# Six staging buffers in place of four for the weight loads of a gated attention block

## The chip, the core and the metric

The kernel runs on one core of a Trainium2 chip. The metric is the device time of one execution in microseconds (us). The engines are PE (TensorE, the matmuls; PEld is its weight load), DVE (VectorE), ACT (ScalarE), POOL (GpSimd) and SP (SyncE). In this kernel SP does no arithmetic: it issues every DMA, one after the other, and waits on semaphores between them.

## What is computed

A gated block on 16 sequences of 64 rows of 256 numbers: attention with 16 query heads in 4 groups of keys and values, and then a gated feed-forward part.

```python
x = x + tanh(g_xattn[0]) * xattn(layernorm(x), ctx, wq, wk, wv, wo, wk_ctx, wv_ctx, q_norm_w, k_norm_w)
x = x + tanh(g_ffn[0]) * ffn(layernorm(x), gate_w, up_w, down_w, gate_scale, up_scale, down_scale)

# xattn: B, L, T = 16, 64, 64; 16 heads of 128, 4 key/value groups
q = rope(rms_norm(x @ wq)); k = rope(rms_norm(x @ wk)); v = x @ wv
k_ctx = rms_norm(ctx @ wk_ctx); v_ctx = ctx @ wv_ctx
probs = softmax(q @ concat(k_ctx, k).T / sqrt(128) + causal mask)
out = (probs @ concat(v_ctx, v)) @ wo

# ffn: weights rounded to float8_e4m3 and back
fuse = silu((x @ gate_w) * gate_scale) * ((x @ up_w) * up_scale)
out = (fuse @ down_w) * down_scale
```

## The kernel before

**Tiles and steps.** Two sequences make a tile of 128 rows, so there are 8 tiles, and 4 steps for each (one group of 4 heads), 32 steps in all. A step number k counts from -6; what comes before step 0 fills the pipeline. Each engine has its own hand-written list of work, in the order of its `one_step`, and runs it strictly in that order; engines wait for one another on semaphores.

**Weights.** They come in 18 chunks, in the order of `CHUNKS`: chunk 0 to 2 are `kv` 0, 1, 2 (context keys, own keys, context values), 3 is `q` 0, 4 is `kv` 3 (own values), 5 and 6 are `q` 1 and 2, 7 is `o` 0, 8 is `q` 3, 9 is `gate` 0, and so on. A `kv`, `q` or `o` chunk has 512 KB, a feed-forward chunk 384 KB. Each lands in the tile `stage`, chunk n in buffer n % RING, and goes from there into its final place: ACT copies it to the high part (`w_kv_hi`, `w_q_hi`, `w_o_hi`, L619), DVE or POOL subtracts to get the low part (L813, L1104), and feed-forward chunks are rounded by DVE (L831 to L850) and stored by POOL (L1115). When that last reader is through, the buffer is free.

**The queue of SP.** Its order is written out by hand. A load of chunk n waits, if n >= RING, for the last reader of chunk n - RING:

```python
if n >= RING:
    before = n - RING
    ...
        sp.wait_ge(w_lo_ready, SPLIT_ORDER.index(CHUNKS[before]) + 1)
```

The list is: the first tile of x (two halves), the context of tile 0, the constants, chunks 0 and 1, seven small loads for the rotary tables and the key weights (L328 to L332), the chunks up to RING - 1, five loads for gates and scales (L336 to L340, semaphore `late_in`), the context of tile 1, the chunks RING and RING + 1, the context of tile 2 (L348), the other 7 tiles of x as two halves of 448 KB (L359, semaphore `x_in`), and then all other chunks in order, with the context of tile 3 ahead of `o` 1:

```python
for n in range(RING, RING + 2):
    load_chunk(n)
load_context(0, 0)
for r in range(2):
    sp.dma_start(x_sb[r * LEN:(r + 1) * LEN, 1:TILES, :], x_by_half[1 - r][:, 1:TILES, :]).then_inc(x_in, 16)
for n in range(RING + 2, len(CHUNKS)):
```

**Who needs what early.** At step -2 DVE waits for `x_in` and counts the statistics of tile 1 (L1030); behind it on DVE stand `w_kv_lo` of `kv` 3 (L813) and all later work. At step -2 PE waits for `late_in` and turns the scale rows (L570); ACT needs the gates at step -1 (L799).

Of the kernel before, what the change touches and what calls it, by code (L numbers as in the profile page):

```python
# [48 lines left out]
SHORT_OF_VECTOR = (3,)  # L49

TABLES_AHEAD_OF = ("kv", 2)
RING = 4
CHUNK_COLS = 1024


# [3 lines left out]
def build(nc, x, ctx_in, g_xattn, g_ffn, wq, wk, wv, wo, wk_ctx, wv_ctx, q_norm_w, k_norm_w,  # L59
# [5 lines left out]
    with ExitStack() as stack:  # L65
        def sb(name, shape, dt=f32):
            return stack.enter_context(nc.sbuf_tensor(name, shape, dt))
# [26 lines left out]
        xn = sb("xn", [P, HID])  # L94
        stage = sb("stage", [P, RING, CHUNK_COLS])
        w_kv = [sb(f"w_kv_{a}", [P, 4, KC, GW], f32r) for a in ("hi", "lo")]
# [178 lines left out]
        def staged(n, cols):  # L275
            return stage[:, n % RING, 0:cols]

# [4 lines left out]
        def _(sp):  # L282
# [10 lines left out]
            def load_chunk(n):  # L293
                kind, i = CHUNKS[n]
                if n >= RING:

                    before = n - RING
                    kind_before, i_before = CHUNKS[before]
                    if kind_before == "o":
                        sp.wait_ge(wo_lo_ready, i_before + 1)  # L300
                    elif kind_before in ("kv", "q"):
                        sp.wait_ge(w_lo_ready, SPLIT_ORDER.index(CHUNKS[before]) + 1)
                    else:
                        sp.wait_ge(quant_done, FF_CHUNKS.index(CHUNKS[before]) + 1)
                if kind == "kv":
                    sp.dma_start(staged(n, CHUNK_COLS).rearrange("p (c n) -> p c n", c=KC), kv_views[i])\
                      .then_inc(chunk_in[n], 16)
                elif kind == "q":
                    sp.dma_start(staged(n, CHUNK_COLS).rearrange("p (c n) -> p c n", c=KC), wq_view[:, i])\
                      .then_inc(chunk_in[n], 16)  # L310
                elif kind == "o":
                    sp.dma_start(staged(n, CHUNK_COLS).rearrange("p (h n) -> p h n", h=HPG), wo_view[:, i])\
                      .then_inc(chunk_in[n], 16)
                elif kind == "down":
                    sp.dma_start(staged(n, FF).rearrange("p (c n) -> p c n", c=FC // 2),
                                 down_view[:, i * (FC // 2):(i + 1) * (FC // 2), :]).then_inc(chunk_in[n], 16)
                else:
                    sp.dma_start(staged(n, FF), ff_views[kind][i * P:(i + 1) * P, :]).then_inc(chunk_in[n], 16)
# [13 lines left out]
            sp.dma_start(k_w_col[:, :], k_norm_w.rearrange("(d a) -> d a", a=1)).then_inc(small_in, 16)  # L332
            for n in range(2, RING):
                load_chunk(n)
# [7 lines left out]
            sp.dma_start(ctx_sb[:, 1, :], ctx_rows[:, 1, :]).then_inc(ctx_in_sem[1], 16)  # L342
            for n in range(RING, RING + 2):
                load_chunk(n)
# [904 lines left out]
```

## Time and profile before

| | |
|---|---|
| median of 3 runs | 347.85 us (347.71 to 348.61) |
| the profiled execution: its time | 348.04 us |
| the profiled execution: its span | 346.5 us |
| PE busy | 295.0 us, 85% of the span |
| DVE busy | 259.7 us, 75% |
| ACT busy | 231.0 us, 67% |
| POOL busy | 203.2 us, 59% |
| read from HBM, written to it | 11.38 MB, 1.05 MB |

Busy time is the union of an engine's instructions, so an engine can be busy for most of the span and still wait at the one place that counts. The time of an execution holds the span and 1.54 us around it. "Landing" of a DMA is the moment at which its completion reaches the semaphore; "us to landing" counts from the start of the issue. The DMA share is the mean busy share of the core's 16 DMA engines; records that overlap can bring it a little above 1.

### The profile page before, as it was taken

What the parts mean: (1) busy time and instruction counts of PE and PEld (TensorE: products, weight loads), DVE (VectorE), ACT (ScalarE), POOL (GpSimd) and SP (SyncE); (2) the same over time, 40 slices, a digit from 0 to 9 for tenths busy, and PEclk for the clock granted to TensorE, in tenths of its full rate; (3) what the DMA queues carried; (4) which work ended last, traced back from release to release, by engine and by line L of the source; (5) the groups of instructions that cost most, each with busy time, mean ns of one, the idle gap of its engine ahead of it and who ended that gap; (6) DMA issues with size and microseconds to landing.
All of it is one profiled execution on the core that took longest, in us unless ns stands there. A gap on an engine that the chain in (4) does not pass through costs nothing.

```text
span 346.5 us, 6537 instructions
## 1 busy us (share of the span) xinstructions
PE 295.0 (85%) x2065; PEld 257.2 (74%) x2065; DVE 259.7 (75%) x576; ACT 231.0 (67%) x886; POOL 203.2 (59%) x193
## 2 busy tenths in 40 slices
PE   1665758589749999999999999999999999988872
PEld 0444646487639889889988898899889988777761
DVE  2557988999899968975897589768976885686452
ACT  3474657566335788688868886887688868775622
POOL 1044759896559665864586458645864585455223
PEclk9989869989887999999999999999999999999998
DMA  6694205021000000000010000000000000000000
GB/s 190 231 295 129 80 29 166 0 93 61 2 0 3 2 15 3 15 3 0 3 30 2 15 0 15 0 0 0 15 0 0 3 16 3 0 2 16 3 15 15
DMA packets 10817, 12.73 MB, mean 37 GB/s; under 512 B 1820, under 2 KB 8232, under 8 KB 10792
## 3 DMA queue, kind: packets, MB, share of 16 engines
q1 hardware_dynamic: 10792, 12.43, 11.9%
q8 instruction: 12, 0.20, 0.2%
q14 instruction: 13, 0.11, 0.1%
HBM read 11.38 MB, written 1.05 MB: 36 GB/s over the span
## 4 chain that ended last, share of the span: by engine, by line
DVE 35%; ACT 26%; issue 17%; POOL 9%; PE 5%; SPq 4%; DMA 3%; POOLq 0%; DVEq 0%; ACTq 0%
ACT probs L792 8%; ACT const L629 7%; DVE row_max L1017 5%; DVE ssq_rows L1049 3%; DMA x_sb<-in_x_dram 3%; DVE q_rot L891 3%; DVE stage L843 3%; ACT tanh_g L683 3%; DVE exp_bias L1020 2%; DVE q_sin L895 2%; ACT values L656 2%; ACT qt L702 2%; POOL q_rot L1152 2%; POOL q_scale L1099 2%; DVE stage L841 2%
## 5 line engine op out<-in xcount | busy, mean ns | idle before, releaser
L792 ACT ACTIVATE probs<-ps_scores,exp_bias,q_scale 128x128 f32<-128x128 f32 x128 | 56.9, 454 | 32.9 <-DVE exp_bias L1020 32.9
L1152 POOL TENSOR_TENSOR q_rot<-q_rot,q_sin 128x512 f32<-128x512 f32 x32 | 42.0, 1311 | 18.1 <-DVE q_sin L895 18.0
L1099 POOL TENSOR_TENSOR q_scale<-ssq_rows,minus_half 128x4 f32<-128x4 f32 x32 | 36.1, 1129 | 24.5 <-DVE ssq_rows L1049 24.5
L410 PE MATMUL ps_y<-w_o_hi,ot_hi 128*128 128x256 f32 x128 | 39.3, 307 | 3.8 <-DVE ot_lo L902 3.8
L1135 POOL TENSOR_TENSOR fuse_lo<-fuse,fuse_hi 128x256 fp32r<-128x256 f32 x22 | 16.1, 732 | 44.5 <-ACT fuse_hi L639 44.5
L1201 POOL TENSOR_TENSOR probs<-probs,row_inv 128x512 f32<-128x512 f32 x32 | 35.9, 1122 | 8.1 <-DVE row_inv L1083 8.1
L629 ACT ACTIVATE const<-ps_q 128x128 bf16<-128x128 f32 x128 | 33.9, 289 | 6.6 <-PE ps_q L384 6.0
L410 PE MATMUL ps_y<-w_o_lo,ot_hi 128*128 128x256 f32 x128 | 37.4, 292 | 0.0
L410 PE MATMUL ps_y<-w_o_hi,ot_lo 128*128 128x256 f32 x128 | 37.3, 292 | 0.0
L556 PE MATMUL ps_scores<-kt,qt 128*128 128x128 f32 x256 | 36.4, 286 | 0.0
L602 PE MATMUL ps_attn<-pt,values 128*128 128x256 f32 x128 | 34.2, 390 | 0.0
L384 PE MATMUL ps_kv<-w_kv_hi,xt_hi 128*128 128x512 f32 x58 | 26.9, 464 | 6.7 <-ACT w_kv_hi L619 3.0
L556 PEld LDWEIGHTS ps_scores<-kt,qt 128*128 128x128 f32 x256 | 32.0, 196 | 0.0
L1049 DVE TENSOR_SCALAR ssq_rows<-ssq 64x2 f32<-64x2 f32 x128 | 30.7, 240 | 1.7
L410 PEld LDWEIGHTS ps_y<-w_o_hi,ot_hi 128*128 128x128 f32 x128 | 25.5, 200 | 8.3 <-DVE ot_lo L902 7.6
L891 DVE TENSOR_TENSOR q_rot<-ps_q,rope 128x512 f32<-128x512 f32 x32 | 21.9, 683 | 11.6 <-ACT const L629 11.4
L769 ACT ACTIVATE pt<-ps_probs 128x512 f32<-128x512 f32 x32 | 19.2, 601 | 17.0 <-PE ps_probs L391 17.0
L902 DVE TENSOR_TENSOR ot_lo<-ps_attn,ot_hi 128x512 fp32r<-128x512 f32 x32 | 22.1, 689 | 11.0 <-ACT ot_hi L695 10.6
L1099 POOL TENSOR_TENSOR k_inv<-k_var,minus_half 128x4 f32<-128x4 f32 x16 | 16.2, 1013 | 21.9 <-DVE k_var L943 21.2
L384 PE MATMUL ps_q<-w_q_hi,xt_hi 128*128 128x512 f32 x64 | 28.7, 449 | 0.3 <-DVE w_q_lo L813 0.3
L629 ACT ACTIVATION_READ_ACCUMULATOR const<-ps_q 128x1 f32 x128 | 27.7, 220 | 0.0
L391 PE MATMUL ps_probs<-const,probs 128*128 128x128 f32 x128 | 20.0, 280 | 8.0 <-POOL probs L1201 8.0
(148 smaller groups left out, 922.6 us busy)
## 6 DMA issues: line engine op xcount, KB each, us to landing
stage<-in_L_xattn_wq_dram SPq DMA_DIRECT2D x4, 512.0 KB, 7.0
stage<-in_L_xattn_wo_dram SPq DMA_DIRECT2D x4, 512.0 KB, 4.7
ctx_sb<-in_ctx_dram SPq DMA_DIRECT2D x8, 128.0 KB, 2.2
out_dram<-x SPq DMA_DIRECT2D x16, 64.0 KB, 1.9
x_sb<-in_x_dram SPq DMA_DIRECT2D x2, 448.0 KB, 8.9
stage<-in_L_ffn_gate_w_dram SPq DMA_DIRECT2D x2, 384.0 KB, 3.2
stage<-in_L_ffn_up_w_dram SPq DMA_DIRECT2D x2, 384.0 KB, 3.0
stage<-in_L_ffn_down_w_dram SPq DMA_DIRECT2D x2, 384.0 KB, 3.6
```

The lines of the kernel that those rows point to most:

```text
L384: last = nc.tensor.matmul(dst, lhs(a, i), rhs(b, i), start=(n == 0), stop=(n == 3 * terms - 1))
L410: last = nc.tensor.matmul(ps_y[:, 0:HID], ot[a][:, h, :], w_o[b][:, g0, h, :], start=(g0 == 0 and n == 0), stop=(g0 == GROUPS - 1 and n == ...
L556: last = nc.tensor.matmul(scores[:, 2 * r + pp, :], qt[:, r, 2 * pp:2 * pp + 2, :], kt[:, par, j, 2 * r:2 * r + 2, :], start=False, stop=( ...
L602: last = nc.tensor.matmul(ps_o[:, r * 256:(r + 1) * 256], values[:, p0, r, g0 * DIM:(g0 + 1) * DIM], pt[:, r * 256:(r + 1) * 256], start=T ...
L629: last = nc.scalar.activation(squares[:, h, :], src[:, h * DIM:(h + 1) * DIM], ACT.Square, accum_out=dst[:, h:h + 1])
L792: last = nc.scalar.activation(probs[:, i, :], ps_s[:, i * P:(i + 1) * P], ACT.Exp, bias=exp_bias[:, i:i + 1], scale=q_scale[:, k % 2, i:i ...
L891: nc.vector.tensor_tensor(q_rot[:, :, :], four(ps_q), over_heads(rope[:, 0, :]), ALU.mult)\
L902: nc.vector.tensor_tensor(ot_lo[:, :, :].rearrange("p h (r l) -> p r h l", r=2), ps_o[:, :].rearrange("p (r h l) -> p r h l", r=2, h=HPG), ...
L1049: last = nc.vector.tensor_scalar(ssq_rows[hh * LEN:(hh + 1) * LEN, 2 * r:2 * r + 2], ssq[r * LEN:(r + 1) * LEN, hh::2], DIM * RMS_EPS, Non ...
L1099: return nc.gpsimd.tensor_tensor(dst, src, minus_half[:, 0:src.shape[1]], ALU.pow)
L1152: nc.gpsimd.tensor_tensor(q_rot[:, :, :], q_rot[:, :, :], q_sin[:, :, :], ALU.add)\
L1201: nc.gpsimd.tensor_tensor(probs[:, :, :], probs[:, :, :], row_inv[:, :].unsqueeze(2).broadcast_to([P, 4, P]), ALU.mult).then_inc(probs_rea ...
```

## The change

```diff
@@ -49,7 +49,7 @@
 SHORT_OF_VECTOR = (3,)
 
 TABLES_AHEAD_OF = ("kv", 2)
-RING = 4
+RING = 6
 CHUNK_COLS = 1024
```

The tile `stage` grows from 4 buffers of 4 KB per partition to 6, and the tiles that are allocated after it move by 8 KB. The lists of PE, DVE, ACT and POOL stay as they are, instruction by instruction; only SP's list changes, since RING stands in its loops and in its waits. Here are three places of the difference on SP.

On SP, right after chunks 2 and 3 (`kv` 2 from `wv_ctx`, `q` 0 from `wq`), ahead of the gates; "+" is what the changed kernel has more at this place:

```order
 L306 DMA stage<-in_L_xattn_wv_ctx_dram 128x2x512
 L309 DMA stage<-in_L_xattn_wq_dram 128x2x512
+L306 DMA stage<-in_L_xattn_wv_dram 128x2x512
+L309 DMA stage<-in_L_xattn_wq_dram 128x2x512
 L336 DMA gates<-in_g_xattn_dram 128x1
 L336 DMA gates<-in_g_ffn_dram 128x1
```

Chunks 4 and 5 (`kv` 3 and `q` 1) now come ahead of the five loads for gates and scales, and wait for nothing.

On SP, the stretch from the last of those five loads to the load of tiles 1 to 7 of x (L359) and a little behind it:

```order
 L340 DMA down_rows<-in_L_ffn_down_scale_dram 128x256
 L342 DMA ctx_sb<-in_ctx_dram 128x256
-L306 DMA stage<-in_L_xattn_wv_dram 128x2x512
 L309 DMA stage<-in_L_xattn_wq_dram 128x2x512
+L312 DMA stage<-in_L_xattn_wo_dram 128x4x256
 L348 DMA ctx_sb<-in_ctx_dram 128x256
 L359 DMA x_sb<-in_x_dram 64x7x256 x2
-L309 DMA stage<-in_L_xattn_wq_dram 128x2x512
-L312 DMA stage<-in_L_xattn_wo_dram 128x4x256
 L309 DMA stage<-in_L_xattn_wq_dram 128x2x512
 L318 DMA stage<-in_L_ffn_gate_w_dram 128x768
```

Chunks 6 and 7 (`q` 2 and `o` 0), which stood behind the load of x, now stand ahead of it. Counted from the start of the list, 8 chunks come ahead of x where 6 did.

On SP, the later loads, with their waits:

```order
 L312 DMA stage<-in_L_xattn_wo_dram 128x4x256 [waits w_lo_ready]
-L312 DMA stage<-in_L_xattn_wo_dram 128x4x256 [waits quant_done]
-L318 DMA stage<-in_L_ffn_up_w_dram 128x768 [waits wo_lo_ready]
+L312 DMA stage<-in_L_xattn_wo_dram 128x4x256 [waits wo_lo_ready]
+L318 DMA stage<-in_L_ffn_up_w_dram 128x768 [waits w_lo_ready]
 L318 DMA stage<-in_L_ffn_up_w_dram 128x768 [waits quant_done]
```

Each later load waits for a chunk two places earlier than it did, so it can be issued earlier; the order of the loads is the same.

## Rows read from the trace of the kernel before

**Rows 1.** The page's first part: busy us (share), instructions.

```profile
PE 295.0 (85%) x2065; PEld 257.2 (74%) x2065; DVE 259.7 (75%) x576; ACT 231.0 (67%) x886; POOL 203.2 (59%) x193
```

**Rows 2.** Chain of waits, 14 to 60 us: start us, us, what.

```profile
14.96 9.64 DMA x_sb<-in_x_dram
...
24.62 0.44 DVE ln_stats L1030
...
26.59 0.60 DVE q_rot L891
27.19 0.61 DVE q_sin L895
...
27.87 2.18 POOL q_rot L1152
```

**Rows 3.** Timeline of DVE: start, us, line, op, [idle before it <- releaser].

```profile
24.62 0.43 DVE L1030 BATCH_NORM_STATS2 ln_stats<-x_sb 128x6 f32<-128x256 f32 x1 [2.64 <-DMA x_sb<-in_x_dram]
```

**Rows 4.** Timeline of SP's DMA issues: start, us, line, target, count.

```profile
8.45 2.09 SPq L336 DMA_DIRECT2D gates<-in_g_xattn_dram  x1
...
12.76 0.43 SPq L306 DMA_DIRECT2D stage<-in_L_xattn_wv_dram  x1
13.23 0.47 SPq L309 DMA_DIRECT2D stage<-in_L_xattn_wq_dram  x1
...
16.39 0.39 SPq L309 DMA_DIRECT2D stage<-in_L_xattn_wq_dram  x1
19.43 0.37 SPq L312 DMA_DIRECT2D stage<-in_L_xattn_wo_dram  x1
```

**Rows 5.** DMA view, a window for each issue: `kv` 3, `q` 2, `o` 0.

```profile
stage<-in_L_xattn_wv_dram SPq DMA_DIRECT2D x1, 512.0 KB, 5.4
...
stage<-in_L_xattn_wq_dram SPq DMA_DIRECT2D x1, 512.0 KB, 9.2
...
stage<-in_L_xattn_wo_dram SPq DMA_DIRECT2D x1, 512.0 KB, 7.4
```

**Rows 6.** The same view for `q` 1 alone.

```profile
stage<-in_L_xattn_wq_dram SPq DMA_DIRECT2D x1, 512.0 KB, 6.6
```

**Rows 7.** Engines by stretch: last three columns are PE clock, DMA share, GB/s.

```profile
8.00:12.00 4.00, 2.05 (x5) 1.70 (x6) 3.01 (x5) 1.60 (x2) 0.00 (x0) 1.00 0.41 107
14.00:16.00 2.00, 1.40 (x4) 0.58 (x2) 0.86 (x1) 1.95 (x9) 0.00 (x0) 1.00 0.68 224
16.00:18.00 2.00, 0.00 (x0) 0.00 (x0) 0.87 (x3) 1.08 (x3) 1.02 (x1) 1.00 1.07 409
19.00:24.00 5.00, 4.53 (x13) 3.23 (x13) 1.77 (x4) 4.33 (x19) 3.07 (x3) 0.67 1.11 239
```

**Rows 8.** Waits, 0 to 130 us: who waited for whom, total us, times, longest.

```profile
ACT w_kv_hi L619 <- DMA stage<-in_L_xattn_wv_ctx_dram: 4.2, 1, 4.2
```

**Rows 9.** Timeline of PE and ACT: scale rows turned, last square of `q` 0.

```profile
18.91 0.28 PE L570 MATMUL ps_y<-const,ff_rows 12*128 12x12 f32 x1
...
23.34 0.22 ACT L629 ACTIVATION_READ_ACCUMULATOR const<-ps_q 128x1 f32 x1
```

**Rows 10.** Chain of waits on PE at its lower granted clock, then that stretch.

```profile
46.90 1.11 PE ps_transposed L391 x4
48.01 2.56 PE ps_kv L384 x6
50.57 1.71 PE ps_attn L602 x4
...
46.20:53.00 6.80, 6.10 (x19) 4.93 (x19) 6.65 (x12) 3.15 (x10) 4.42 (x3) 0.50 0.00 0
107.60:340.00 232.40, 222.31 (x1718) 198.03 (x1717) 173.84 (x428) 171.60 (x677) 138.14 (x141) 1.00 0.02 7
```

**Rows 11.** Timeline of PE at the full granted clock: six matmuls of 512 columns, the first and the end.

```profile
59.02 0.40 PE L384 MATMUL ps_kv<-w_kv_hi,xt_hi 128*128 128x512 f32 x1
...
60.41 1.02 PE L602 MATMUL ps_attn<-pt,values 128*128 128x256 f32 x4
```

## The prediction, written before the changed kernel ran

> **What bounds the kernel now.** I read four views. The page's busy times say only that no engine is bound everywhere: PE is busy for 85% of the span and DVE for 75% [rows 1]. So the place decides, and the chain of waits is next. Between 14 and 60 us its longest link by far is no engine: it is the load of tiles 1 to 7 of x, whose second half is issued at 14.96 us and lands 9.64 us later, at 24.60. It releases the statistics of tile 1 on DVE, and from there the chain runs without a hole through DVE (`q_rot`, `q_sin`) to POOL and on [rows 2]. The timeline of DVE shows the price: DVE stood still for 2.64 us before that instruction, and its releaser is this DMA [rows 3]. What stands behind it on DVE can't start earlier, since an engine works its list in order.
>
> The third view is who waits for a weight chunk, which is what a deeper ring could mend. In the first 130 us the one wait of weight is that of `w_kv_hi` for chunk 2 (`wv_ctx`): 4.2 us, once [rows 8]. Chunk 2 is loaded without any wait for a buffer, by both rings and at the same place of SP's list. For a chunk that the ring held back, from chunk 4 on, no wait of an engine is in that list. The fourth view is the queue itself: it is nearly always full. The DMA share is 1.07 from 16 to 18 us, at 409 GB/s, and 1.11 from 19 to 24 us; only 8 to 12 us (0.41) and 14 to 16 us (0.68) are light [rows 7].
>
> So the weights have slack, and the load of x has none. The change shifts the two against each other.
>
> **Later loads: nothing.** From chunk 8 on, each load waits for a chunk two places earlier and can start sooner. No engine waits for those chunks in the trace, so an earlier landing buys nothing; I cost it at 0. The lists of all compute engines are the same. The moved addresses of other tiles I cost at 0 too: nothing in the trace shows an instruction whose time hangs on its address, for gain or for loss.
>
> **Chunks 4 and 5 ahead of the gate loads: nothing on the path.** They are in front of x in either kernel, so for x only their order among the small loads changes. They land earlier by what is now behind them, and nobody waited for them [rows 8]. The five small loads land later, by two chunks. They stood ahead of chunk 4 in the queue, whose landing is 12.76 + 5.4 = 18.16 us [rows 4, 5], so they were in by then; with up to 3.3 us more (below) it is 21.5 us at the worst. PE turned the scale rows at 18.91 us [rows 9], so PE may slip by up to 2.6 us there. What follows on that path is the projection of `q` 0, whose squares ended at 23.34 + 0.22 = 23.56 us on ACT [rows 9]; with 2.6 us more it is 26.2 us. DVE uses them in `q_rot`, at 26.59 us before [rows 2] and later now. The cover is the wait for x; without it, 3.0 us of slack remain, still more than 2.6.
>
> **Chunks 6 and 7 ahead of x: the term that counts.** The load of x stands in the same queue, and now 1 MB more stands ahead of it. SP comes first: its issue of x moves by two DMA instructions of 0.39 and 0.37 us, so under 1 us with the gaps [rows 4]. The buffers of chunks 0 and 1, for which chunks 6 and 7 wait, are those for which chunks 4 and 5 waited before, and these were issued at 12.76 and 13.23 us, 0.43 and 0.47 us each, one right behind the other: those waits were over [rows 4]. The 2.09 us of the issue at 8.45 us [rows 4] has no cause in the trace. If it happens a second time, x is issued at some 17.3 us. Even that costs nothing, since the turn of x in the queue comes later: before it was behind chunk 5, which landed at 13.23 + 6.6 = 19.83 us [rows 4, 6], and now it is 2.5 us or more later still.
>
> Then the service time of two chunks, from landings that follow one another in a full queue. `kv` 3 landed at 18.16 us and `q` 1 at 19.83: 1.67 us a chunk. `q` 2 landed at 16.39 + 9.2 = 25.59 us and `o` 0 at 19.43 + 7.4 = 26.83: 1.24 us [rows 4 to 6]. Two chunks are between 2.5 and 3.3 us. The throughput gives the same: 1.049 MB at 409 GB/s are 2.6 us [rows 7]. From this I take off nothing or a part of the 2 x 0.32 = 0.64 us that lay idle from 14 to 16 us [rows 7], in case a longer queue ahead fills it. That makes 1.9 to 3.3 us, and I take 2.7, near the upper of the measured rates, as the queue is full where the two chunks now run. The Trainium skill (DMA: Bandwidth & Descriptors, Specifications) gives about 358 GB/s as the limit of HBM for one core; by it the two chunks would take an estimated 2.9 us. The trace disagrees, as it has 409 GB/s over 2 us.
>
> **Does a later x arrive in full at the end?** DVE stood idle before the statistics, so it has nothing to catch up with: all of the shift goes into that wait, which grows from 2.64 to about 5.3 us. Behind it DVE works without a gap until 27.80 us and POOL takes over [rows 2]. What ACT and PE do meanwhile was done before DVE needed it. From 107.6 to 340 us the pattern is periodic, with PE busy for 222.31 of 232.40 us [rows 10], so there is no slack in which a late start would vanish. I pass it on one to one.
>
> **The sum.** 348.04 us of the profiled execution + 2.7 = 350.7 us. That execution was 0.19 us above the median of the runs, so against 347.85 us it is 350.5 us, 0.8% slower.
>
> **Rival 1: the light stretches absorb the move.** From 8 to 12 us the DMA engines were busy for 0.41 only, so 4.0 x 0.59 = 2.4 us lay idle, and 0.64 us from 14 to 16 [rows 7], together 3.0 us, more than the two chunks need. If chunks 4 and 5 fill them, since they are issued at 8.4 us now, x lands where it did, and the time is 347.85 us. For it: they are at hand at the right moment. Against it: chunk 2 and chunk 3 were at hand as well, issued before 8.45 us, and the engines stayed light. The queue seems to be held by the small loads ahead of them, and that stays. Only the 14 to 16 us part can really shrink. A rule leads to the same side: the Trainium skill (Trainium Kernel Development and Optimization, Best Practices) asks to double-buffer, so that DMAs overlap with compute. By that rule more buffers could only help or do nothing. The trace disagrees here, as no engine waits for a buffer's chunk and all 18 share a queue with x. Chance of within 0.3%: 0.13.
>
> **Rival 2: faster, by PE's clock.** From 46.2 to 53.0 us PE's granted clock was 0.50, so 1.2 GHz, and PE was the chain: six matmuls of keys took 2.56 us and four of attention 1.71 [rows 10]. At the full 2.4 GHz the six ran from 59.02 to 60.41, 1.39 us, and the four in 1.02 [rows 11]. That is 1.9 us, and with the turned tiles around them some 2.6 us. A shift of all work by 2.7 us moves it against these low stretches. If this one went away, the time would be 347.9 us; to get below 346.8 us it has to give back over 3.7 us, which needs a second such stretch on the chain, for some 346.3 us. For it: PE's pause before 26 us grows, and low stretches came after busy ones. Against it: the order of pauses and work after x is the same, only shifted, and the later low stretches are beside DVE's work. It ends on the other side from over 3.7 us. Chance: 0.07.
>
> **Rival 3: worse.** x itself goes slowly: from 19 to 24 us the engines were busy at 1.11 and moved only 239 GB/s [rows 7]. If chunk 8, now issued right behind x, or one more low stretch of PE's clock (up to 1.7 us, half of some 3.4 us) adds to it, the time is 351.2 to 352.7 us. Chance: 0.13.
>
> **How the numbers follow.** My forecast, 350.5 us with a range of its own from 349.7 to 351.2, has 0.60; part of rival 2 that only gives back 1 to 2 us lies between 348.9 and 349.7, with 0.07. So slower by over 0.3% (1.04 us, about what a measurement of this kernel can tell from no change) has 0.60 + 0.07 + 0.13 = 0.80, within it 0.13, faster 0.07. The range of 348.5 to 352.2 us leaves out faster (0.07), most of rival 1 (0.10) and the tail of rival 3 (0.02).
>
> **What would show it.** In the changed kernel's trace: DVE's wait before L1030 at 5.0 to 5.6 us, and its start at 27.1 to 27.6 us; chunks 6 and 7 landed by about 23 us; no new wait for a chunk; POOL's `q_rot` of step 0 at about 30.6 us in place of 27.87; the same distance from there to the end. The prediction is wrong if the statistics start below 25.7 us (rival 1), or if they start late and the end doesn't move (clock, rival 2).

## The result: 1.4% slower, by 4.6 us where 2.7 were forecast

| | before | after |
|---|---|---|
| median of 4 runs each | 348.0 us (347.71 to 348.61) | 352.62 us (351.64 to 354.23) |
| ratio, 95% interval | | 1.0139 [1.0111, 1.0167] |
| the profiled execution: its time | 348.04 us | 352.51 us |
| the profiled execution: its span | 346.5 us | 351.0 us |
| start of the statistics of tile 1 (L1030) | 24.62 us | 27.83 us |
| start of `q_rot` of step 1 (L891) | 33.66 us | 38.19 us |
| from there to the end of the span | 312.81 us | 312.79 us |

The direction was right and the size was not: 352.62 us lies above the range of 348.5 to 352.2 us. The table already holds the account of the 4.5 us of span. 3.21 us have arisen when the statistics of tile 1 start, 1.32 more between there and `q_rot` of step 1, and nothing after it. That is how the loss is divided in these two executions; other traces of the same orders, below, divide it otherwise.

The page's busy times (us, share, instructions) tell as little as before [rows 1]. All are within 0.5 us of the old ones:

```profile
PE 295.5 (84%) x2065; PEld 257.4 (73%) x2065; DVE 259.7 (74%) x576; ACT 230.8 (66%) x886; POOL 203.2 (58%) x193
```

The chain of waits of the changed kernel, 16 to 40 us (start, us, what), answers to [rows 2]:

```profile
16.82 10.99 DMA x_sb<-in_x_dram
...
27.83 0.44 DVE ln_stats L1030
...
29.80 0.60 DVE q_rot L891
30.40 0.61 DVE q_sin L895
...
31.07 2.19 POOL q_rot L1152
...
33.30 1.11 PE ps_transposed L391 x4
34.42 2.57 PE ps_q L384 x6
...
37.02 1.15 ACT const L629 x8
...
38.19 0.63 DVE q_rot L891
```

It is the same chain. Its longest link is still the second half of x, now 10.99 us long and issued 1.86 us later. From the statistics to POOL's `q_rot` the distance is 3.24 us, before it was 3.25. Then the two kernels part: PE turns the four tiles of `q` in 1.11 us and projects step 1 in 2.57 us. The chain of the kernel before has the turned tiles and `q_rot` of step 1 like this:

```profile
30.10 0.67 PE ps_transposed L391 x4
...
33.66 0.52 DVE q_rot L891
```

From the start of the turned tiles to `q_rot` of step 1 it was 3.56 us and is now 4.89. The windows of the changed kernel (us; busy PE, PEld, DVE, ACT, POOL; then PE clock, DMA share, GB/s) show why, and what the queue does:

```profile
16.00:18.00 2.00, 0.00 (x0) 0.00 (x0) 1.00 (x2) 1.63 (x7) 0.92 (x1) 0.73 1.03 351
19.00:24.00 5.00, 5.00 (x15) 3.81 (x16) 2.41 (x4) 3.57 (x17) 2.29 (x2) 0.52 1.08 284
...
30.60:37.40 6.80, 5.79 (x18) 4.19 (x17) 3.77 (x10) 2.05 (x6) 3.19 (x2) 0.50 0.00 0
112.60:345.00 232.40, 222.14 (x1719) 198.02 (x1718) 173.36 (x428) 171.90 (x677) 137.81 (x142) 1.00 0.03 7
```

From 30.6 to 37.4 us PE's granted clock was 0.50, its level of 1.2 GHz, and in that stretch lie the two pieces of the chain that are PE's. The kernel before did the same work at 2.4 GHz; its low stretch came at 35.9 to 39.4 us, behind them. The last row answers to the last one of [rows 10]: the long middle, shifted by 5 us, is as dense as before.

DVE's timeline (start, us, line, op, idle before and its releaser) answers to [rows 3]:

```profile
27.83 0.43 DVE L1030 BATCH_NORM_STATS2 ln_stats<-x_sb 128x6 f32<-128x256 f32 x1 [4.94 <-DMA x_sb<-in_x_dram]
```

And SP's issues (start, us, line, target, count), with the landings of chunk 6 and 7 and of x in the DMA view (KB each, us to landing), answer to [rows 4, 5]:

```profile
8.45 2.42 SPq L306 DMA_DIRECT2D stage<-in_L_xattn_wv_dram  x1
...
14.55 0.44 SPq L309 DMA_DIRECT2D stage<-in_L_xattn_wq_dram  x1
15.04 0.47 SPq L312 DMA_DIRECT2D stage<-in_L_xattn_wo_dram  x1
...
16.11 2.19 SPq L359 DMA_DIRECT2D x_sb<-in_x_dram  x2
```

```profile
stage<-in_L_xattn_wq_dram SPq DMA_DIRECT2D x1, 512.0 KB, 6.5
...
stage<-in_L_xattn_wo_dram SPq DMA_DIRECT2D x1, 512.0 KB, 8.3
...
x_sb<-in_x_dram SPq DMA_DIRECT2D x2, 448.0 KB, 10.0
```

Chunk 6 landed at 14.55 + 6.5 = 21.0 us and chunk 7 at 15.04 + 8.3 = 23.3 us. The list of waits (total us, times, longest) names no chunk that the ring could have held back, as before [rows 8]:

```profile
DVE ln_stats L1030 <- DMA x_sb<-in_x_dram: 8.5, 2, 4.9
...
ACT w_kv_hi L619 <- DMA stage<-in_L_xattn_wv_ctx_dram: 4.6, 1, 4.6
```

### The profile page after: what moved, and what is told of

Same layout as the page of the kernel before. It is cut to its first block, busy times and chain, and to the rows that moved or that the text cites. A ratio compares the mean times of both kernels' runs of the same rounds, so it can differ in the third digit from the quotient of the medians.

```text
span 351.0 us, 6537 instructions
## 1 busy us (share of the span) xinstructions
PE 295.5 (84%) x2065; PEld 257.4 (73%) x2065; DVE 259.7 (74%) x576; ACT 230.8 (66%) x886; POOL 203.2 (58%) x193
## 4 chain that ended last, share of the span: by engine, by line
DVE 36%; ACT 25%; issue 17%; POOL 8%; SPq 4%; PE 4%; DMA 3%; POOLq 0%; DVEq 0%; ACTq 0%
ACT probs L792 8%; ACT const L629 7%; DVE row_max L1017 5%; DVE ssq_rows L1049 4%; DMA x_sb<-in_x_dram 3%; DVE q_rot L891 3%; DVE stage L843 3%; ACT tanh_g L683 3%; DVE exp_bias L1020 3%; DVE q_sin L895 2%; ACT qt L702 2%; POOL q_rot L1152 2%; POOL q_scale L1099 2%; DVE stage L841 2%; ACT values L656 2%
## 5 line engine op out<-in xcount | busy, mean ns | idle before, releaser
L1201 POOL TENSOR_TENSOR probs<-probs,row_inv 128x512 f32<-128x512 f32 x32 | 35.9, 1122 | 8.1 <-DVE row_inv L1083 8.1
L602 PE MATMUL ps_attn<-pt,values 128*128 128x256 f32 x128 | 33.3, 382 | 0.0
L891 DVE TENSOR_TENSOR q_rot<-ps_q,rope 128x512 f32<-128x512 f32 x32 | 21.9, 684 | 13.0 <-ACT const L629 12.9
L410 PEld LDWEIGHTS ps_y<-w_o_hi,ot_hi 128*128 128x128 f32 x128 | 25.5, 199 | 7.7 <-DVE ot_lo L902 7.0
L1099 POOL TENSOR_TENSOR k_inv<-k_var,minus_half 128x4 f32<-128x4 f32 x16 | 16.2, 1012 | 22.7 <-DVE k_var L943 21.9
```

The lines of the kernel that those rows point to most:

```text
L410: last = nc.tensor.matmul(ps_y[:, 0:HID], ot[a][:, h, :], w_o[b][:, g0, h, :], start=(g0 == 0 and n == 0), stop=(g0 == GROUPS - 1 and n == ...
L602: last = nc.tensor.matmul(ps_o[:, r * 256:(r + 1) * 256], values[:, p0, r, g0 * DIM:(g0 + 1) * DIM], pt[:, r * 256:(r + 1) * 256], start=T ...
L891: nc.vector.tensor_tensor(q_rot[:, :, :], four(ps_q), over_heads(rope[:, 0, :]), ALU.mult)\
L1099: return nc.gpsimd.tensor_tensor(dst, src, minus_half[:, 0:src.shape[1]], ALU.pow)
L1201: nc.gpsimd.tensor_tensor(probs[:, :, :], probs[:, :, :], row_inv[:, :].unsqueeze(2).broadcast_to([P, 4, P]), ALU.mult).then_inc(probs_rea ...
```

## The experiments

Twelve kernels ran, in three groups of four on one chip each. The kernel before ran beside them: 348.42 us (median of 19 runs) beside the first group, 348.19 (15) beside the second, 348.25 (13) beside the third. A ratio is taken over the runs of both kernels and stands with its 95% interval; it need not be the quotient of the two medians. In all tables, "stats" is the start of the statistics of tile 1, "to q_rot" the time from there to `q_rot` of step 1, and "rest" from there to the end of the span, all from the profiled execution.

### First group: which part of the change costs the time

**Six buffers, the old order of loads.** From the changed kernel:

```diff
-            for n in range(2, RING):
+            for n in range(2, 4):
...
-            for n in range(RING, RING + 2):
+            for n in range(4, 6):
...
-            for n in range(RING + 2, len(CHUNKS)):
+            for n in range(6, len(CHUNKS)):
```

> Six buffers, but SP's loads in exactly the order of the kernel before (chunks 4 and 5 behind the gate loads, chunks 6 and 7 behind the load of x); only addresses and the later waits on buffers differ from before. Theory (the place of the load of x in the queue): no change, 347.7 to 348.6 us, statistics of tile 1 on DVE start at 24.4 to 25.0 us. Rival (the moved tiles or the earlier later loads cost something): 350 us or more.

**Chunks 4 and 5 early, 6 and 7 behind x again.**

```diff
-            for n in range(RING, RING + 2):
-                load_chunk(n)
...
-            for n in range(RING + 2, len(CHUNKS)):
+            for n in range(6, len(CHUNKS)):
```

> The changed kernel with the load of x back ahead of chunks 6 and 7; chunks 4 and 5 stay ahead of the gate loads. Theory: x lands at 24.6 to 25.2 us, 347.8 to 348.8 us, the low stretch of PE's clock back at about 36 us. Rival (chunks 4 and 5 ahead of the gate loads, which make PE late, take part of the 4.5 us): 349.5 us or more.

**Half the dose: only chunk 6 ahead of x.**

```diff
-            for n in range(RING, RING + 2):
+            for n in range(6, 7):
...
-            for n in range(RING + 2, len(CHUNKS)):
+            for n in range(7, len(CHUNKS)):
```

> The changed kernel with the load of x between chunks 6 and 7: half the dose. Theory: x lands 1.4 to 1.7 us later than before, at 26.0 to 26.4 us; by that alone 349.5 us, and 350.8 us if PE's clock is low at the projection for step 1 as well. Rival (the cost is of another kind): 352 us as the changed kernel, or 348.

**The change once more, as it is.**

> The changed kernel once more, for a second trace of it. Theory: x lands at 27.2 to 27.9 us, PE's clock is low from about 30.6 us, 351.6 to 353 us, and the work behind step 1 is shifted by a constant. Rival (the clock or the landing fell so by chance in the first trace): another place of the low stretch with another time.

| | median us (runs) | ratio | stats | to q_rot | rest |
|---|---|---|---|---|---|
| old order | 348.47 (10) | 1.0000 [0.9988, 1.0012] | 25.60 | 9.04 | 313.06 |
| 6 and 7 behind x | 348.65 (10) | 1.0012 [0.9999, 1.0025] | 24.03 | 9.04 | 313.51 |
| only 6 ahead | 350.50 (4) | 1.0065 [1.0039, 1.0091] | 25.92 | 9.09 | 313.53 |
| the change | 353.14 (4) | 1.0141 [1.0087, 1.0194] | 28.78 | 9.42 | 313.54 |

The first row settles that the buffers themselves, their addresses and the earlier issue of all later loads cost and bring nothing beyond 0.12%. The second settles the same for chunks 4 and 5 ahead of the gate loads. So the whole loss belongs to chunks 6 and 7 ahead of x. One of them costs 2.1 us, two cost 4.7. The change's second trace is not a copy of the first: the statistics start at 28.78 us, later than the 27.2 to 27.9 expected, the way to `q_rot` costs 0.38 us more than before and not 1.32, and the rest is 0.7 us longer than in either profiled execution of the result. The timelines of DVE of these two kernels show it in the same place, chunks 6 and 7 behind x and then one of them ahead:

```profile
24.03 0.43 DVE L1028 BATCH_NORM_STATS2 ln_stats<-x_sb 128x6 f32<-128x256 f32 x1 [2.08 <-DMA x_sb<-in_x_dram]
```

```profile
25.92 0.43 DVE L1030 BATCH_NORM_STATS2 ln_stats<-x_sb 128x6 f32<-128x256 f32 x1 [3.46 <-DMA x_sb<-in_x_dram]
```

### Second group: does lateness alone do it, and what is next behind x

**The kernel before, with DVE made late.** After the wait for `x_in`, DVE does four operations that nothing reads; no load moves.

```diff
                         dve.wait_ge(x_in, 32)
+                        for i in range(4):
+                            nc.vector.tensor_scalar(idle[:, :], as_f32(w_kv[0][:, 0].rearrange("p c n -> p (c n)")),
+                                                    1.0, None, ALU.mult).then_inc(idle_done, 1)
+                            dve.wait_ge(idle_done, i + 1)
```

> The kernel before, with four extra instructions on DVE between the wait for x and the statistics of tile 1, some 3.2 us together; no load is moved. It costs the late start by itself. Theory (a late start of the statistics passes on one to one, with up to 1.3 us of PE's clock on top): 351.0 to 353 us. Rival (the loads and not the late start cost the time, so that a part of the start is absorbed): below 350.5 us.

It took 352.05 us (4 runs), 1.0099 [1.0076, 1.0123], so some 3.5 us more. Its DVE timeline:

```profile
24.33 3.69 DVE L1033 TENSOR_SCALAR idle<-w_kv_hi 128x1024 f32<-128x1024 f32 x4 [1.32 <-DMA x_sb<-in_x_dram]
28.05 0.43 DVE L1036 BATCH_NORM_STATS2 ln_stats<-x_sb 128x6 f32<-128x256 f32 x1
```

x came as early as ever, and the statistics started 3.43 us later than in the kernel before. From there to `q_rot` of step 1 it was 9.51 us in place of 9.04. So a late start, with not one load moved, is passed on in full, and brings a part of PE's term with it (0.47 us here). A late start of DVE is enough by itself for a loss of this kind.

**The changed kernel with PE filled.** PE does 14 matmuls that nothing reads while it waits for tile 1.

```diff
+                if at_step(u, k) == -1:
+                    for _ in range(14):
+                        nc.tensor.matmul(ps_s[:, :], xt[0][:, 0, 0, :], w_kv[0][:, 0, 0, :], start=True, stop=True)
                 if at_step(u, k) != -2:
                     keys_values(u, k)
```

> The changed kernel, with 14 extra matmuls of 512 columns on PE into the unused bank of the scores, in the pause in which PE waits for the late statistics; their results are not used. Theory (the pause lets PE's clock fall, and the projection for step 1 then runs at 1.2 GHz): x lands as late as before the edit, but the transposes and the projection from 33 to 38 us run at the full clock, and 0.4 to 1.3 us of the loss come back: 351.3 to 352.2 us. Rival (the clock has no part): as the changed kernel, 352.6 to 353.1 us.

It took 354.45 us (4 runs), 1.0168 [1.0141, 1.0195]: slower than the changed kernel, which neither theory had said. The timeline of PE shows why it could not decide:

```profile
26.08 3.45 PE L589 MATMUL ps_scores<-w_kv_hi,xt_hi 128*128 128x512 f32 x14
31.76 0.62 PE L384 MATMUL ps_probs<-w_kv_hi,xt_hi 128*128 128x512 f32 x1 [2.23 <-DVE w_kv_lo L816]
...
35.12 1.11 PE L391 MATMUL ps_transposed<-const,q_rot 128*128 128x128 f32 x4 [0.61 <-POOL q_rot L1155]
```

The fill ended at 29.53 us, PE stood still for 2.23 us after all, and its clock was at 1.2 GHz from 31.9 to 38.75 us. Besides, x landed only at 29.6 us. The fill was too short, and it is repeated below.

**Tile 1 of x on its own, early.** Its two halves of 64 KB go ahead of the context of tile 1; tiles 2 to 7 stay where x was, with a semaphore of their own that DVE waits for at tile 2. Once from the changed kernel and once, with the same edit, from the kernel before:

```diff
+            for r in range(2):
+                sp.dma_start(x_sb[r * LEN:(r + 1) * LEN, 1, :], x_by_half[1 - r][:, 1, :]).then_inc(x_in, 16)
             sp.dma_start(ctx_sb[:, 1, :], ctx_rows[:, 1, :]).then_inc(ctx_in_sem[1], 16)
...
-                sp.dma_start(x_sb[r * LEN:(r + 1) * LEN, 1:TILES, :], x_by_half[1 - r][:, 1:TILES, :])\
-                  .then_inc(x_in, 16)
+                sp.dma_start(x_sb[r * LEN:(r + 1) * LEN, 2:TILES, :], x_by_half[1 - r][:, 2:TILES, :])\
+                  .then_inc(x_rest_in, 16)
...
                         dve.wait_ge(x_in, 32)
+                    if isinstance(u, int) and tile(u, m + 2) == 2:
+                        dve.wait_ge(x_rest_in, 32)
```

> The changed kernel with tile 1 of x (two halves of 64 KB) loaded by itself ahead of the context of tile 1, and tiles 2 to 7 where the load of x was. Theory: the wait of DVE before the statistics of tile 1 (2.64 us before) goes, so 345.0 to 346.5 us, six buffers or four. Rival (next on DVE is kv 3 or the squares of q 0, close behind): 347 us or more.

> The same edit on the kernel before, with four buffers. Theory: as the one with six buffers within 0.3%, since no engine waits for a chunk from 4 on; 345.0 to 346.5 us. Rival (a deeper ring helps once x is out of the way): over 0.5 us slower than with six.

| | median us (runs) | ratio | stats | to q_rot | rest |
|---|---|---|---|---|---|
| DVE late | 352.05 (4) | 1.0099 [1.0076, 1.0123] | 28.05 | 9.51 | 313.30 |
| PE filled, 14 | 354.45 (4) | 1.0168 [1.0141, 1.0195] | 29.65 | 10.36 | 312.87 |
| tile 1 early, six buffers | 347.30 (10) | 0.9968 [0.9952, 0.9984] | 22.96 | 9.05 | 313.40 |
| tile 1 early, four buffers | 347.19 (7) | 0.9958 [0.9939, 0.9977] | 22.81 | 9.05 | 313.66 |

Both are faster than the kernel before, and alike. Both missed their expectation of 345.0 to 346.5 us; their rival, that the next limit is close behind, had 347 or more for the first of them and held. With six buffers, two chunks still stand ahead of the bulk of x, and it costs nothing any more, since nobody waits for that bulk. So the loss of the change is nothing but one small piece of data, tile 1, that travels at the end of a large queue. The gain is only some 1.1 to 1.5 us, because the next limit is close: DVE no longer waits for a DMA, but for the squares of the keys, and those go back to chunk 2. The timeline of ACT with four buffers:

```profile
14.61 1.06 ACT L621 ACTIVATE w_kv_hi<-stage 128x1024 fp32r<-128x1024 f32 x1 [4.77 <-DMA stage<-in_L_xattn_wv_ctx_dram]
```

### Third group: the clock, the size of pieces, and chunk 2

**The kernel before, once more.**

> The kernel before once more, for a second trace of it with the same order of loads. Theory: statistics of tile 1 start at 24.3 to 25.6 us, 9.0 us to the rotation of step 1 where PE's clock is full, 347.7 to 348.7 us. Rival (the first trace was one with an early x by luck): above 25.6 us.

**Another chunk in place of `o` 0.** `o` 0 comes in pieces of 1 KB, `q` 3 like `q` 2 in pieces of 2 KB. Chunks 6 and 8 go ahead of x:

```diff
-            for n in range(RING, RING + 2):
+            for n in (6, 8):
...
-            for n in range(RING + 2, len(CHUNKS)):
+            for n in (7, *range(9, len(CHUNKS))):
```

> The changed kernel with chunks 6 and 8 (both of 256 pieces of 2 KB) ahead of the load of x, and chunk 7 (o 0, 512 pieces of 1 KB) behind it. Theory (the two chunks cost more than forecast because the pieces of o 0 are small): the statistics of tile 1 start at 27.2 to 27.6 us in place of 27.8 to 29.7, 351 to 352 us. Rival (any chunk ahead of x costs the same, and the spread is that of the DMA engines): 27.8 to 29.7 us and 352.5 to 353.2 us.

**The changed kernel with PE filled for longer.** The edit of the 14 matmuls, with 26.

> As the filled PE, with 26 extra matmuls in place of 14, so that PE is busy until x lands. Theory (the pause right before lets the clock fall): the distance from the statistics to the rotation of step 1 is 9.0 to 9.5 us in place of 10.4, and 352.0 to 353 us. Rival (work in the pause doesn't keep the clock, or slows the load of x): 354 us or more with 9.5 us or more.

**Chunk 2 ahead of the small loads as well.** The kernel before with tile 1 of x early, and:

```diff
-            load_chunk(0)
-            load_chunk(1)
+            for n in range(3):
+                load_chunk(n)
...
-            for n in range(2, RING):
-                load_chunk(n)
+            load_chunk(3)
```

> The version with tile 1 of x early and four buffers, with chunk 2 ahead of the seven small loads for the rotary tables as well; ACT waited 4.8 us for that chunk. Theory (the place in the queue is what counts, and now the small loads become late instead, since the squares on ACT wait for the tables): 346.4 to 347.4 us, a gain of at most 0.8 us. Rival (chunk 2 alone bound the start): 343.5 to 345.5 us.

| | median us (runs) | ratio | stats | to q_rot | rest |
|---|---|---|---|---|---|
| before again | 348.45 (10) | 0.9999 [0.9982, 1.0016] | 24.06 | 9.05 | 312.68 |
| `q` 3 in place of `o` 0 | 352.41 (4) | 1.0103 [1.0081, 1.0126] | 28.09 | 9.51 | 313.57 |
| PE filled, 26 | 352.25 (4) | 1.0104 [1.0087, 1.0121] | 29.32 | 9.04 | 312.82 |
| chunk 2 early too | 346.41 (4) | 0.9937 [0.9919, 0.9955] | 22.45 | 9.05 | 313.24 |

The size of the pieces is not the cause: with `q` 3 the statistics start at 28.09 us, as late as with `o` 0 (27.83 and 28.78). The time, 352.41 us, lies between the two forecasts and does not decide by itself. The kernel before, once more, had its statistics at 24.06 us, a little earlier than the 24.3 to 25.6 expected.

The longer fill decides on the clock. Its PE timeline, fill, then step -1's values, then the turned tiles and two of the six matmuls of step 1; behind it DVE's row:

```profile
25.42 6.18 PE L589 MATMUL ps_scores<-w_kv_hi,xt_hi 128*128 128x512 f32 x26
31.44 0.46 PE L384 MATMUL ps_probs<-w_kv_hi,xt_hi 128*128 128x512 f32 x1
...
34.79 0.66 PE L391 MATMUL ps_transposed<-const,q_rot 128*128 128x128 f32 x4 [1.73 <-POOL q_rot L1155]
35.20 0.48 PE L384 MATMUL ps_q<-w_q_hi,xt_hi 128*128 128x512 f32 x1
...
36.44 0.39 PE L384 MATMUL ps_q<-w_q_hi,xt_lo 128*128 128x512 f32 x1
```

```profile
38.36 0.69 DVE L894 TENSOR_TENSOR q_rot<-ps_q,rope 128x512 f32<-128x512 f32 x1 [2.39 <-ACT const L632]
```

x was as late as with the short fill (29.32 against 29.65 us), but there was no pause before step -1's matmuls, the clock stayed at 2.4 GHz, and the way to `q_rot` took 9.04 us in place of 10.36. That is the 1.32 us of the changed kernel, given back, and with the 0.33 us of x it is the difference of the spans, 352.9 and 351.2 us. These are single traces, but the mean granted clock of every execution says the same. With 26 matmuls it was 0.954 to 0.964 in the four runs, as in the kernel before (0.951 to 0.960 in the ten runs of this group). In the kernels with a late start and no fill, or too short a one, it was lower: 0.943 to 0.947 in the change, 0.939 to 0.950 in its repetition, 0.938 to 0.946 with `q` 3, 0.943 to 0.947 with DVE late and with 14 matmuls.

The last kernel is the fastest, 0.6% below the kernel before. ACT now has chunk 2 at 10.4 us in place of 14.6, and the next wait is for the rotary tables, whose small loads it overtook:

```profile
10.40 1.06 ACT L620 ACTIVATE w_kv_hi<-stage 128x1024 fp32r<-128x1024 f32 x1 [0.26 <-DMA stage<-in_L_xattn_wv_ctx_dram]
15.30 0.28 ACT L630 ACTIVATE const<-ps_kv 128x128 bf16<-128x128 f32 x1 [3.83 <-DVE rope L861]
```

## Why the prediction missed: the steps one by one

**"The weights have slack, and the load of x has none": right.** No chunk is newly waited for, and the wait for x is where the loss starts. The two kernels with tile 1 early confirm it from the other side.

**Later loads, addresses, chunks 4 and 5: nothing, right.** 1.0000 [0.9988, 1.0012] and 1.0012 [0.9999, 1.0025]. PE turned the scale rows at 19.92 us, 1.0 us later, and the last square of `q` 0 ended at 24.24 us, 5.6 us before DVE wanted it. The long issue stood at the same 8.45 us again, now before chunk 4 and 2.42 us long. The issue of x moved by 1.86 us, where the prediction had under 1 us for the two instructions ahead of it and 17.3 us as the worst start; it was harmless, as supposed, since the first completion of chunk 7, the last chunk ahead of x, came at 20.7 us only.

**Two chunks ahead of x, taken at 2.7 us from a range of 1.9 to 3.3: too small.** That is the first term that failed. The statistics started 3.21 us later in the profiled execution, and by the other traces of that order it is more. The step at fault is the service time of a chunk, taken from one landing to the next as 1.24 to 1.67 us, and from 409 GB/s. In the changed kernel chunk 5 landed at 18.5 us, chunk 6 at 21.0 and chunk 7 at 23.3: some 2.5 and 2.3 us each, though between 5 and 6 the five small loads and a context stand as well. The queue was full and moved 351 GB/s from 16 to 18 us and 308 from 18 to 20. Two things lowered the bill: chunk 5 landed 1.3 us earlier than before, as chunks 4 and 5 filled the light stretch (14 to 16 us: 403 GB/s in place of 224 [rows 7]), and x followed the last chunk after 4.5 us in place of 4.8. That is 4.9 - 1.3 - 0.35 = 3.2 us.

A load releases its reader with its last completion. The semaphore of x counts 32 of them, 16 for each half; the first, the middle one (the 17th) and the last, in us:

| chunks ahead of x | traces | first | middle | last |
|---|---|---|---|---|
| 6 | before, before again, six buffers in the old order, DVE late | 20.8 to 21.6 | 22.9 to 23.6 | 24.0 to 25.6, mean 24.6 |
| 6 | 6 and 7 behind x (4 and 5 early) | 19.6 | 22.0 | 24.0 |
| 7 | only 6 ahead | 21.5 | 23.8 | 25.9 |
| 8 | after, the change again, `q` 3 for `o` 0 | 22.7 to 22.9 | 25.0 to 26.2 | 27.8 to 28.8, mean 28.2 |
| 8 | PE filled, 14 and 26 | 22.6 to 22.7 | 26.0 to 26.1 | 29.3 to 29.6 |

Against the old order the middle completion comes 2.3 us later on average (23.2 to 25.5 us), the last one 3.6. Against the second row, which differs from the changed kernel in chunks 6 and 7 alone, it is 3.4 and 4.2 us, with one trace there. So 2.7 us was near the middle completion only because chunks 4 and 5 had brought x forward, and DVE waits for the last. The spread from first to last is 3.2 to 4.0 us in the old order, 4.4 in the second row and the third, 4.9 to 6.1 in the fourth. In the kernel before, the 32 fall into two groups of 16, from 21.40 to 22.45 and from 23.31 to 24.60 us; the changed kernel has no such gap. A single chunk shows it without two halves: the 16 completions of chunk 7 lie 0.7 us apart in the kernel before and 2.7 in the changed one. The Trainium skill (DMA: Bandwidth & Descriptors, Queues, rings and completion order) says that a copy is split over rings on up to 16 DMA engines and that each works through its own in order; by its section on why a DMA increments its semaphore by 16 and not by 1, only the full count of completions means that all has landed. The trace agrees: the statistics start 0.02 us after the last of the 32, 2.6 us after the middle one. Nothing shows why the completions drift apart; it is not the number of chunks alone, as the second row has 6 ahead like the first.

**"I pass it on one to one": right for the load, but a term was missing.** From `q_rot` of step 1 on, the distance to the end is the same to 0.02 us. So close a match is luck: over all fourteen traces it is 312.7 to 313.7 us, and 313.54 in the change's other trace. But no late start is made up behind that point, as that step said, and DVE late, with no load moved, shows the same. Ahead of that point PE ran at 1.2 GHz. This second term was 1.32 us in the profiled execution, 0.38 in the change's other trace, 0.46 with `q` 3 and 0.47 with DVE late. With 3.21 us for the chunks alone the execution would have taken 348.04 + 3.21 = 351.25 us, inside the range; it is this term, left out of the sum, that carried it beyond. The prediction had it, but inside rival 3, as one of three ways to be worse with 0.13 in all and "up to 1.7 us". It should have stood in the sum, since the change lengthens the very pause that comes before PE's next burst.

**Rival 2 had the clock, but read it the wrong way round.** It held that "low stretches came after busy ones". In the experiment with 26 matmuls PE was busier, and the low stretch on the chain went away. What PE did before is in its timelines, here of the kernel before and then of the changed one:

```profile
26.74 0.47 PE L384 MATMUL ps_probs<-w_kv_hi,xt_hi 128*128 128x512 f32 x1 [1.76 <-DVE w_kv_lo L813]
```

```profile
29.95 0.47 PE L384 MATMUL ps_probs<-w_kv_hi,xt_hi 128*128 128x512 f32 x1 [4.06 <-DVE w_kv_lo L813]
```

After a pause of 1.76 us (and of 1.47 with six buffers in the old order, 1.20 with 6 and 7 behind x, 0.51 in the kernel before again) step 1's projection ran at 2.4 GHz. After 4.06 us (2.23 with the short fill) the clock fell to 1.2 GHz within the next microseconds; with 4.84 us in the change again, 4.44 with `q` 3 and 4.16 with DVE late it fell during the pause. With only chunk 6 ahead the pause was 2.57 us, and the low stretch, 28.1 to 31.5 us, ended just as the turned tiles, at 31.40, had begun: it cost 0.05 us. So where the low stretch lies decides what is lost, and that differs from run to run.

**Rival 1, the light stretches, fell.** x did move by far more than nothing. Its reason against it held: from 8 to 12 us, where the seven small loads are ahead, the queue stayed light (123 to 127 GB/s), and only the stretch from 14 to 16 us filled up.

**Rival 3, what it named beside the clock.** Chunk 8 right behind x is no difference between the kernels: in the kernel before, chunk 6 stood there, issued 0.51 us after x. That x itself goes slowly held (below), but in both kernels.

**The signs.** DVE's wait 4.94 us (5.0 to 5.6 named), its start 27.83 (27.1 to 27.6), chunks 6 and 7 at 21.0 and 23.3 (by about 23), POOL's `q_rot` 31.07 (30.6), and the distance from there to the end 319.9 us, before it was 318.6. The last is the sign that pointed at the missing term.

**The range.** It reached to 352.2 us and cut the tail of rival 3. The two terms at their upper ends, 3.3 for the chunks and 1.7 for PE, make 348.04 + 5.0 = 353.0 us. They aren't independent, as a later x makes the longer pause, so their sum belonged inside. The change's second trace shows that even 3.3 was no upper end: there the statistics started 4.2 us later than in the profiled execution of the kernel before.

## What to carry to other kernels

More buffers in a ring also let its loads go earlier, and where one queue carries everything, something else goes later: look first for whoever stands behind them in that queue and is waited for, and send the one small piece that is due first ahead on its own (here 128 KB, for 0.3 to 0.4%, and 0.6% with chunk 2 moved up too). Price a place in the queue by the last completion, in traffic like that which will stand there, and not by the best rate in the trace: two chunks taken at 2.7 us cost 3.2 to 4.2. And where a change lengthens a pause of PE ahead of work on the chain, put the lower clock on that work into the sum, not among the rivals.

## What the runs showed of the chip

- **x is slow wherever it stands in the queue.** The windows of the changed kernel, 22 to 24 and 24 to 26 us, when x is what moves:

```profile
22.00:24.00 2.00, 2.00 (x7) 1.56 (x6) 0.17 (x1) 1.60 (x13) 1.77 (x2) 0.56 1.12 235
24.00:26.00 2.00, 1.49 (x8) 0.77 (x6) 0.00 (x0) 1.99 (x5) 1.04 (x1) 1.00 1.10 242
```

  The DMA engines are busy throughout and move 235 to 242 GB/s, against 409 with weights [rows 7]; in the kernel with 6 and 7 behind x it is 226 and 238 from 18 to 22 us. In the packet records a piece of 1 KB takes about 77 ns there, and 46 to 55 in the five microseconds before; a piece of 2 KB of the weights beside it takes 140 ns in place of 84. The Trainium skill (SBUF — State Buffer, Door 1: The DMA port swizzle) says that partitions 0 to 63 reach only 8 of SBUF's 16 DMA ports, with 196 GB/s measured for them. Each half of x goes to 64 partitions. The measured 235 to 242 GB/s, with some other traffic in it, is nearer to that figure than to 409, and no run tells this cause from others.
- **The long issue stayed where it was when the load there changed.** In both kernels the 16th DMA of SP's list, issued at 8.45 us, took long: 2.09 us for the gates, 2.42 us for chunk 4. With chunk 2 ahead of the small loads the 16th took 0.47 us and the 17th, at 9.33 us, 1.21. Its cause is not shown.
- **PE can lose clock by resting.** 26 unused matmuls kept it at 2.4 GHz, and the way to `q_rot` took 9.04 us, 0.38 to 1.32 less than in the traces of the change. Little of it is left in the time (1.0104 [1.0087, 1.0121] against 1.0139 [1.0111, 1.0167]), as x came later in both kernels with a fill.

**Open.** Why the completions of x spread by 3.2 us in one trace and by 6.1 in another; it is not the size of the pieces of `o` 0, as `q` 3 gave 5.3. Whether PE's work slows x: with a fill it landed at 29.3 and 29.6 us, without one at 27.8 to 28.8, in two traces and three. And why the low stretch of PE's clock starts at another moment in each execution of one kernel, which makes the second term 1.32 us once and 0.38 the other time.
